# A four-layer graph network on one core: in the third layer GpSimd fetches two of six tiles in every batch

## What is computed

```python
x = _layernorm(x + _L0_gnn_ref(x, src, dst, ...))        # attention over the edges
x = _layernorm(x + _L1_gnn_ref(x, edge_index, W))        # relu((x + sum of neighbours) @ W)
x = _layernorm(x + _L2_gnn_ref(x, edge_index, edge_attr_4, ...))
x = _layernorm(x + _L3_gnn_ref(x, edge_index, edge_type_64, ...))
```

```python
x_agg = silu(x[src] @ agg_W + agg_b) * e_w               # e_w: one weight for each edge
out = segment_sum(x_agg, dst, num_segments=n)
```

## Time and profile before

| | |
|---|---|
| median of 3 runs | 1096.84 us (1095.36 to 1097.76) |
| the profiled execution's own time | 1096.41 us |
| its span, first to last instruction | 1094.6 us |
| third layer's gather and scatter on PE | 731.2 to about 974 us |
| fetches by GpSimd | 158, from 731.25 to 965 us |

### The profile page before, as it was taken

The page is one execution under the profiler, slowest core; times in us unless marked ns, Lnnn a source line. Parts: engine busy times, 40 slices in busy tenths (PEclk is TensorE's granted clock), DMA queues, the critical chain, the costliest instruction groups (busy, mean ns, idle before and its releaser), DMA issues.

```text
span 1094.6 us, 27898 instructions
## 1 busy us (share of the span) xinstructions
PE 1010.9 (92%) x10463; PEld 869.1 (79%) x10463; DVE 862.6 (79%) x1934; ACT 694.1 (63%) x1489; POOL 217.1 (20%) x260
## 2 busy tenths in 40 slices
PE   4797979699999999995999999779999999989997
PEld 3343557699999999994777778769999999976765
DVE  6775999988998989987766677778787888766754
ACT  3466755455545555556777788577677776776554
POOL 4401240000000000000000000226766666610000
PEclk9898998899999999997999999889999999999998
DMA  6000020477767677643766564245444445434232
GB/s 158 1 1 1 4 68 3 129 214 219 237 216 232 217 222 236 221 147 104 254 191 192 171 181 149 67 120 142 127 138 139 124 136 135 115 108 127 69 98 83
DMA packets 86924, 150.38 MB, mean 137 GB/s; under 512 B 14523, under 2 KB 58374, under 8 KB 86556
## 3 DMA queue, kind: packets, MB, share of 16 engines
q1 hardware_dynamic: 65609, 116.01, 35.6%
q10 hardware_dynamic: 16122, 22.16, 5.6%
q0 software_dynamic: 5056, 10.36, 3.8%
HBM read 112.56 MB, written 35.94 MB: 136 GB/s over the span
## 4 chain that ended last, share of the span: by engine, by line
PE 82%; DVE 10%; ACT 4%; issue 2%; DMA 1%; POOL 0%; POOLq 0%; DVEq 0%; SPq 0%; ACTq 0%
PE PS L2496 14%; PE PS L2696 14%; PE PS L2484 11%; PE PS L2679 8%; PE PS L2607 7%; PE PS L2782 6%; PE PS L2575 4%; PE PS L2582 3%; PE PS L2322 2%; PE PS L2335 2%; PE PS L2399 2%; DVE vo L1659 1%; DVE ring L1655 1%; ACT X L1223 1%; PE PS L2353 1%
## 5 line engine op out<-in xcount | busy, mean ns | idle before, releaser
L1147 ACT CAST vo<-XT 128x768 f32<-128x768 bf16 (+1 forms) x218 | 180.3, 827 | 163.2 <-PE PS L2696 64.1
L980 POOL DMA_INDIRECT XT<-tab,ring x158 | 160.0, 1013 | 112.2 <-PE PS L2696 60.7
L2496 PE MATMUL PS<-vo 128*128 128x133 f32 x1300 | 175.9, 284 | 1.2 <-ACT vo L1147 1.2
L2496 PEld LDWEIGHTS PS<-vo 128*128 128x128 f32 x1300 | 157.2, 191 | 1.3 <-issue 1.3
L2484 PE MATMUL PS<-kp,ring 128*128 128x132 bf16 x1950 | 146.6, 221 | 3.2 <-DVE ring L1627 1.7
L2696 PE MATMUL PS<-vo 128*128 128x128 f32 x984 | 132.8, 279 | 0.0
L2484 PEld LDWEIGHTS PS<-kp,ring 128*128 128x128 bf16 x1950 | 125.6, 97 | 5.4 <-DVE ring L1627 1.8
L1637 DVE TENSOR_TENSOR XT<-iotab,XT 128x768 bf16<-128x768 bf16 (+1 forms) x218 | 119.9, 550 | 3.0 <-ACT XT L1137 1.6
L2696 PEld LDWEIGHTS PS<-vo 128*128 128x128 f32 x984 | 118.9, 191 | 3.0 <-issue 2.4
L1282 ACT CAST adjf_r<-PS 128x512 fp32r<-128x512 f32 (+1 forms) x175 | 94.2, 543 | 27.4 <-PE PS L2575 25.2
L2486 PE MATMUL PS<-SDP,ring 128*128 128x12 bf16 x650 | 110.2, 170 | 0.0
(11 more groups left out here) (350 smaller groups left out, 2046.0 us busy)
## 6 DMA issues: line engine op xcount, KB each, us to landing
ring<-rows_d SPq DMA_DIRECT2D x146, 416.0 KB, 5.8
hots_d<-XT ACTq DMA_DIRECT2D x108, 192.0 KB, 4.7
big<-hots_d SPq DMA_DIRECT2D x10, 640.0 KB, 4.5
XT<-hots_d SPq DMA_DIRECT2D x10, 640.0 KB, 4.7
adj_d<-ring SPq DMA_DIRECT2D x20, 320.0 KB, 2.4
big<-hots_d SPq DMA_DIRECT2D x8, 480.0 KB, 4.1
adj_d<-ring SPq DMA_DIRECT2D x15, 240.0 KB, 2.1
ring<-adj_d SPq DMA_DIRECT2D x11, 320.0 KB, 3.2
```

The source lines that it names most:

```text
L980: G.indirect_dma_start(far_rows[:, f % FBUF, :], None, tab[2], bass.IndirectOffsetOnAxis(ap=far_row[:, t:t + 1], axis=0)).then_inc(far_in[ ...
L1147: C.copy(ohd[:, k % 3, 0:n, :], ohb[:, k % 3, 0:n, :]).then_inc(hots_wide, 1)
L2496: T.matmul(bank(6 + b % 2)[:, 0:VW], ohd[:, k % 3, i, :], vals[:, k % 3, i, :], start=j == 0, stop=j == JN - 1).then_inc(scattered, 1)
```

## The change

In every full batch from the fourth on the last two tiles are far, in even batches as in odd ones. `far_tiles`, the waits on `gathered_up` (through `near_until`) and all loops over `near(k)` and `far(k)` follow from `near`. There are 210 far tiles then and 440 near ones.

```diff
     def near(k):
-        return batch(k)[:BT - 1 - k % 2] if k >= 3 and len(batch(k)) == BT else batch(k)
+        return batch(k)[:BT - 2] if k >= 3 and len(batch(k)) == BT else batch(k)
```

## The result

| | before | after |
|---|---|---|
| median | 1096.53 us (6 runs, 1095.36 to 1098.64) | 1140.6 us (6 runs, 1138.15 to 1144.74) |
| ratio | | 1.0404, 95% interval 1.0389 to 1.0419 |
| profiled execution, its span | 1096.41, 1094.6 us | 1140.28, 1138.5 us |
| first and last far scatter starts on PE | 741.7, 972.9 us | 740.9, 1015.3 us |

The account below looks back on a forecast made before the run. PE bounds the stage before; after the change POOL's fetches do. Fetch 8 at 742.33, 201 intervals of 1.313, landing and scaling shift the last far pair +36.6 us: 1094.6 + 36.6 + 1.8, plus 0.4, gives 1133.4; range 1119 to 1158.

Parts of the forecast that it names:

- fetch 8 starts: POOL's fetch 8, counted from 0, still waits for the first far scatter at 741.7 and starts at 742.33 us.
- 201 intervals: From fetch 8 to the last, number 209, POOL starts one each 1.313 us; bounds 1.255 and 1.418.
- landing and scaling, to the last far scatter: After the last fetch starts, 2.9 us to land and ACT's 0.40; PE's last far pair begins at 1009.5.
- PE and DVE: In 52 batches PE loses 8.8 us of matmuls; DVE's multiply loses 7.1 us, hidden already and worth nothing.
- ACT: ACT scales 52 more tiles, 20.5 us, hidden in its 61 us free in the stage.
- POOL: 52 more fetches: four a pair of batches need 5.02 us against PE's 4.12, so POOL sets the end.
- none waited longer than 0.3 us: No POOL fetch waited longer for the landing four before it; used to bound landing at four intervals, 5.02 us.
- a landing past 5 us: Sign of a wrong prediction: POOL then waits for its own DMAs; the interval is a quarter of start to landing.
- Moves with it: The short last batch, end of the update and fourth layer shift with the last far scatter, +36.6 us.
- PE stays the bound: Rival: POOL issues a far tile each 1.03 us and the stage loses 8.8 us: 1088 us; 5%.
- Collisions in every batch, or in none: Rivals: DVE's comparisons always lengthen a fetch, 1154.6 us, 25%; or always miss, 1121 to 1123 us, 13%.
- The clock: Rival: PE's pauses lower its clock for a tenth of the stage's batches, costing 15 us: 1148 us; 5%.

Follow-up runs that it names:

- the second experiment: Changed kernel with two instead of three gather matmuls for each near tile; 1143.11 us in one run.
- the fifth: Changed kernel with two far tiles in odd batches and none in even ones, 106 fetches; 1103.91 us, ratio 1.0068 to the kernel before.
- first experiment: Changed kernel with DVE's bf16 comparisons of the third layer cut to a few columns; 1132.35 us, ratio 1.0337 to the kernel before.
- with more room: Ten buffers and eight landing semaphores instead of eight and four: changed kernel 1135.57 us; with 175 fetches 1094.46 us, ratio 0.9979 to the kernel before.

## Why the prediction was right, step by step

The forecast was 1133.4, the measurement 1140.6, within the stated range. The span moved by 43.9 us where 36.6 was forecast. The direction, the new bound and the wait were right; sizes were off. The terms of the sum, in the profiled executions:

| term | forecast | measured | difference |
|---|---|---|---|
| fetch 8 starts | 742.33 | 741.57 | −0.8 |
| 201 intervals | 263.9 (1.313 each) | 269.8 (1.342) | +5.9 |
| landing and scaling, to the last far scatter | 3.3 | 3.9 | +0.6 |
| from there to the end of the span | 121.7 | 123.2 | +1.5 |
| span | 1131.2 | 1138.5 | +7.3 |

**PE and DVE.** 8.8 us of matmuls and 7.1 us of multiplying left their engines and were worth nothing. The first is shown: 24.6 us more taken from PE changed nothing in the second experiment, and while PE is the bound, in the fifth, a tile is worth its matmuls. That DVE's part is worth nothing was argued from its slack alone.

**ACT.** The 20.5 us of more scaling were hidden, as far as slack can say: ACT waits 78.5 us for landings in front of it. No run takes the scaling away.

**POOL.** Right in kind: the queue's own gap of 0.30 us, not in the busy time, is what puts the fetch over the 1.03 us that PE allows. The interval was mis-sized by 0.029 us. That is two errors of opposite sign, and that they partly cancelled is luck. The mean fetch was 0.997 us, not 1.013 (−3.2 us over 201). The gap averaged 0.345, not 0.30 (+9.0): eleven late landings make 6.4 of it, the pause of fetch 113 1.7, the rest is that the smallest gap is 0.304. The step that failed is "none waited longer than 0.3 us", from which I took landings never to hold POOL up. The waits of that row were the smallest gap itself. At 158 fetches four intervals were long enough for it (four times 1.49 us on average from fetch 8 on); with fetches at 1.34 us a landing of 5.9 us is longer than four of them. The prediction named the sign, a landing past 5 us, but gave it no price. With these waits gone the interval was 1.309, the forecast's 1.313 almost to the point.

**Landing.** Mis-sized by 0.6 us. About half of it is the landing: 2.9 from plain loads of the same size, where the last fetch took 3.2 us:

```profile
1011.38 3.24 DMA XT<-tab,ring
...
1014.64 0.03 ACT XT L1314
```

The other half is reading: the last start in the earlier trace rows is that of the last tile's second matmul, some 0.2 us behind the first, and the prediction took it for the beginning of the pair. The earlier trace rows was also too narrow. It shows two of the rows of 64 KB on SP's queue, the quickest and one at 2.9, and the same view has others, the longest of them this:

```profile
b<-in_L_gnn_W_b SPq DMA_DIRECT2D x1, 64.0 KB, 5.1
```

So the plain loads took from 2.4 to 5.1 us, and nothing in them singled out 2.9.

**What follows the stage.** "Moves with it" was off by 1.5 us. PE's first matmul of the fourth layer came 2.95 us after the last far scatter before (975.85 against 972.9) and 3.2 us after it now (1018.49 against 1015.3). It waited then as now, for another engine:

```profile
975.85 0.47 PE L2782 MATMUL PS<-adjf_r,xh_r 128*128 128x512 f32 x1 [1.39 <-DVE xl_r L2123]
```

```profile
1014.64 0.40 ACT L1314 ACTIVATE XT<-XT,EWS 128x128 f32<-128x128 f32 x1 [0.95 <-DMA XT<-tab,ring]
...
1015.09 0.49 PE L2696 MATMUL PS<-vo,XT 128*128 128x128 f32 x2 [0.81 <-ACT XT L1314]
...
1018.49 0.47 PE L2782 MATMUL PS<-adjf_r,xh_r 128*128 128x512 f32 x1 [1.60 <-ACT adjf_r L1419]
```

So only 0.2 us went there. Most of the rest is lost in the first 15 us of the fourth layer, in which PE was busy for 12.66 us before and 11.77 now (busy time from that matmul on, before and after):

```profile
975.85:990.85 15.00, 12.66 (x55) 8.84 (x56) 9.65 (x31) 11.51 (x23) 0.00 (x0) 1.00 0.50 147
```

```profile
1018.49:1033.49 15.00, 11.77 (x51) 8.07 (x52) 9.01 (x30) 11.47 (x22) 0.00 (x0) 1.00 0.46 137
```

Why the fourth layer starts with more pauses was not tried.

**The rivals.** PE stays the bound: no, since the gap of 0.30 never shrank. Collisions in every batch, or in none: neither, since the mean fetch is 0.997 and 46 of 210 were long; that they cost at all is right (first experiment). The clock: it did fall a little (0.99 over the stage), and at 0.96 in the second experiment the time still went with POOL.

## To carry to other kernels

An engine's room for more work is its interval, not its busy time: find a stretch of the time line in which it waited for nothing, take start to start, and multiply. Where work moves from a full engine to one at 88%, move only up to the crossing. Here 17 tiles of the 52, with more room, gave 0.2%, and one half of them, 26, without it already cost 1.2%; where the crossing lies between was not tried. A row that says that nobody waits for a landing holds for the old distance between transfers; when the distance shrinks, it has to be asked again, and a few more semaphores and buffers gave back 5 of the 44 us here.

## What the hardware showed that was not expected

- A fetch of 128 rows of 512 bytes by indirect DMA takes 0.945 us of GpSimd and a gap of 0.30 us that is there even when nothing is waited for; with 64 rows it takes 0.903 (medians). The cost is by the fetch, hardly by the row.
- The landing of such a fetch came 3.0 us after its start in the median (2.5 to 4.7, with more room), and in the changed kernel up to 5.9 us after. What delays it these runs don't show.
- In the changed kernel a fetch beside one of DVE's bf16 comparisons was lengthened in 45 of 132 cases, up to 1.37 us, and mostly ended a fixed time (about 0.12, 0.35 or 0.82 us) after the comparison did.
- With pauses of PE of 0.3 us a batch and more the granted clock fell only now and then: it averaged 0.99 and 0.96 over two stages in which PE was busy for 89% and 83% of the time.
